# A two-layer sequence kernel: reciprocals of the softmax denominators stored once and repeated by a copy within DRAM

## Chip, cores and metric

The kernel runs on one core of a Trainium2 chip. The metric is the device time of one execution in microseconds (us). A core has a matrix engine (TensorE, "PE" in the profile, its weight loads "PEld"), a vector engine (DVE), a scalar engine (ACT), a general engine (GpSimd, "POOL") and a sequencer that issues nearly all transfers here (SyncE, "SP"). Transfers run on 16 DMA engines. "DRAM" is the chip's memory outside the core; on-chip tiles have 128 partitions.

## What is computed

Eight sequences (B = 8) of S = 512 rows by D = 256 pass through two layers. Layer 0 is a feed-forward block with one of eight weight sets for each sequence, a residual and a layer norm. Layer 1 is a conditioned transformer block with H = 16 heads of 16 columns. Cut to what the change touches:

```
scores = einsum('bhqd,bhkd->bhqk', q / sqrt(16), k) + attention_bias   # bias: 8 x 16 x 512 x 512 floats
probs  = softmax(where(src_mask, -inf, scores), axis=-1)
ctx    = einsum('bhqk,bhkd->bhqd', probs, v)
x      = x + (ctx @ Wo + bo)
h      = layernorm(x) * g2 + beta2
out    = x + gelu2(h @ W1 + b1) @ W2 + b2
```

The kernel does not divide `probs`. It sums exp(scores) through a 17th column of ones in `v`, so that `ctx` comes out undivided beside its denominators, and multiplies `ctx` by the reciprocals of the denominators later.

## The kernel before, in words

There are three stages. The first (about 0 to 260 us) is layer 0 and the projections to q, k and v. The second is the attention: N = 512 tiles, that is 128 units (a batch and a head) of 4 tiles of 128 query rows. All engines walk the same step number n. In step n PE makes the scores of tile n (L714, for every fourth unit with a second matmul L712), DVE adds the bias and finds the row minimum (L1257), ACT takes the exponential (L940), PE turns tile n-4 (L725, the constant LAG is 4), ACT or DVE copies it out of PSUM (L830, L1267), and later PE makes the context of four heads at once (L738). POOL adds the mask to the bias tile of three units in four, in two halves (L1455).

The third stage (from about 805 us) takes the batches one by one: POOL multiplies context by reciprocals (`divide`, L1491), ACT and POOL split the product in two parts (`high_c`, `low_c`), PE projects it (`project`), DVE adds the residual and norms, PE runs the two feed-forward matmuls (`up`, `down2`), and SP stores the output. PE's order in it is written out by hand: `up(b)`, `project(b + 2)`, three of four `down2(b)`, the turn of batch b + 1, the last `down2(b)`.

SP issues its transfers in one written order too, and a wait in it holds all that stands behind. `attention_loads(n)` is what it issues in step n. Those that matter here:

- `load_bias(u)`: 1 MB for unit u, 128 rows of 8 KB, into one of NB = 5 buffers. It stands in step 4(u - 3) and waits until PE has turned the last tile of unit u - 5, tile 4u - 17, which PE does in its step 4u - 13.
- `load_qk(g, i)`: q and k for a group of 8 units (32 tiles), in four pairs, in steps 4, 10, 16 and 22 of the 32 tiles before.
- `store_ctx(gi)`: in step 16 gi + 37, five transfers. Context of four heads to `sc_c` and the four rows of denominators to `sc_d`.
- For each batch b: `load_den(b)` in step 64 b + 97 loads the 16 x 512 denominators as a tile of 128 x 64; DVE takes reciprocals into `rr` (L1272); `store_rec(b)` in step 64 b + 111 writes `rr` to `sc_r[b]`, laid out [2, 16 columns, 8 heads, 512], which holds each reciprocal 16 times, once for each column of its head. It does so in two transfers (k = 0 and 1), each with 64 partitions of `rr` as source, 16 times over, 256 bytes a piece: 1024 pieces, 256 KB.
- `load_ctx(b)` loads `sc_c[b]` to `t_cin` and `sc_r[b]` to `t_din`, both 128 x 1024 (two pieces of 2 KB for each partition), waiting on the semaphore `d_rs` between the two. Batch 0's stands in step 486, batch 1's in step 498, batches 2 and 3 after step 515, batches 4 to 7 in the loop over the output batches. `load_x2(b)` brings the residual `t_rin`.

Batches 0 to 6 have `store_rec` in the second stage, batch 7 in the third. In the profile all of these stand as line L276, the helper `load`; they are told apart by their tensors. The shape of the source and destination lists is that of the lines quoted here:

```
for k in range(NK):
    load(d_rs, sc_r[b, k].rearrange("d h (c q) -> (h c) d q", c=8), rr[64 * k:64 * k + 64, :].unsqueeze(1).broadcast_to([64, HD, H * S // 128]))
```

Of the kernel before, what the change touches and what calls it, by code (L numbers as in the profile page):

```python
# [5 lines left out]
F32 = mybir.dt.float32  # L6
# [8 lines left out]
B, S, D, I, H, HD = 8, 512, 256, 1024, 16, 16  # L15
NT = S // 128
NK = D // 128
# [48 lines left out]
def kpn(a):  # L66
    return a.rearrange("(k p) n -> p k n", p=128)
# [41 lines left out]
def masks(u, half):  # L109

    return 2 * sum(on_pool(i) for i in range(u)) + half + 1


def program(nc, x, x_t, itok, tstep, bias, mask, Wi, bi, Wo0, bo0, gam, bet, Wada, bada, Wq, bq, Wk, bk, Wv, bv,
            Wo, bo, W1, b1, W2, b2, g2, be2, ident, freqs, out):
    with ExitStack() as ctx:

        def sem(name):
            return ctx.enter_context(nc.semaphore(name))

        def dram(name, shape, dt):
            return nc.dram_tensor(name, shape, dt, kind="Internal").ap()

        def sbuf(stack, name, shape, dt=F32):
            return stack.enter_context(nc.sbuf_tensor(f"t_{name}", shape, dt))
# [8 lines left out]

        sc_c = dram("sc_c", [B, NK, HD, H // NK, S], F32)

        sc_d, sc_r = dram("sc_d", [B, H, S], F32), dram("sc_r", [B, NK, HD, H // NK, S], F32)


        d_id, d_it, d_c, d_w, d_xt, d_wi, d_wo, d_v, d_ss, d_ssb = (sem(f"d_{n}") for n in ("id", "it", "c", "w", "xt", "wi", "wo", "v", "ss", "ssb"))  # L140
# [2 lines left out]
        d_p = [[sem(f"d_p{p}{n}") for n in range(2)] for p in range(2)]  # L143
        d_b = [sem(f"d_b{i}") for i in range(NB)]
        d_q, d_m, d_vb, d_cs = ([sem(f"d_{n}{i}") for i in range(2)] for n in ("q", "m", "vb", "cs"))
        d_cw, d_rb, d_dn, d_rs = (sem(f"d_{n}") for n in ("cw", "rb", "dn", "rs"))
        d_l, d_r, d_out = ([sem(f"d_{n}{i}") for i in range(2)] for n in ("l", "r", "out"))
        p_hid, p_down, p_x2T, p_q, p_v, p_emb = (sem(f"p_{n}") for n in ("hid", "down", "x2T", "q", "v", "emb"))
        a_gelu, a_hTh, a_xTh, a_wih, a_woh, a_x2Th, a_p0, a_p1, a_wsm, a_sin = (
# [21 lines left out]
        with ExitStack() as st:  # L171
# [20 lines left out]
            stt, mv, rs = sbuf(st, "stt", [128, NT, 6]), [sbuf(st, f"mv{i}", [128, NT, 2]) for i in range(2)], [sbuf(st, f"rs{i}", [128, NT]) for i in range(2)]  # L192
# [12 lines left out]
        with ExitStack() as st:  # L205
# [17 lines left out]
            dn, rr = (sbuf(st, n, [128, H * S // 128]) for n in ("dn", "rr"))  # L223
            ws = {"o": (Wo, NK, D), "1": (W1, NK, I), "2": (W2, NM, D)}
            wl = {n: [sbuf(st, f"cw{n}{p}", [128, k, w], F32R) for p in "hl"] for n, (_, k, w) in ws.items()}
            rb, b1c = sbuf(st, "rb", [128, 4, D]), sbuf(st, "b1c", [128, NM])
# [45 lines left out]
        def sync_program(e):  # L272
            P = Port(e)

            def load(signal, dst, src):
                e.dma_start(dst, src).then_inc(signal, 16)  # L276
# [80 lines left out]
            def store_part(b, n, a, mt):  # L357

                if a == 0:
                    P.wait_ge(a_p0, 4 * b + 2 * n + mt + 1)  # L360
                elif a == 1:
                    P.wait_ge(a_p1, 2 * b + n + 1)
                else:
                    P.wait_ge(g_p2, 2 * b + n + 1)
                g = slice(a, NP3, 3) if n else slice(3 * a, min(3 * a + 3, NP3))
                k = len(range(NP3)[g])
                load(d_p[b % 2][n], sc_qk[b, n, mt, g].rearrange("i p s -> p i s"), parts[b % 2][n][:, a:a + 1, mt, :].broadcast_to([128, k, S]))
# [26 lines left out]
            def load_bias(u):  # L394
                if u >= NB:
                    P.wait_ge(p_T, 4 * (u - NB) + 4)
                load(d_b[u % NB], bt[u % NB][:, :, :], bias[u // H, u % H])

            def load_qk(n, i):

                b, half = divmod(n, 2)
                hs = slice(2 * i, 2 * i + 2)
                P.wait_ge(p_sc, 32 * (n - 1))
                if b < 2 or n < 4:
                    for w in range(2):
                        P.wait_ge(d_p[b % 2][w], PT * (b // 2 + 1))
                for dst, w in ((qs, 0), (ks, 1)):
                    load(d_q[n % 2], dst[n % 2][:, hs, :], sc_qk[b, w, half].rearrange("i (d h) s -> (i d) h s", d=HD)[:, hs, :])
# [39 lines left out]
            def first_stage_over():  # L448
                P.wait_ge(v_v, 4 * B)
                P.wait_ge(g_p2, 2 * B)  # L450
                P.wait_ge(v_x2Tl, NK * B)

            def attention_loads(n):
                nonlocal nextb
                while nextb < min(UNITS, n // NT + NB) and n >= 4 * (nextb - NB) + 3 + LAG + 1:
                    load_bias(nextb)
                    nextb += 1
                if n in late_stores:
                    i = late_stores.index(n)
                    store_part(B - 1, i // 2 % 2, i // 4, i % 2)  # L460
                if n == 88:
                    first_stage_over()
                    for w in range(2):
                        P.wait_ge(d_p[0][w], PT * B // 2)
                    P.wait_ge(d_v, 16 * B)
                    P.wait_ge(d_x2[0], 16 * B // 2)
                    P.wait_ge(d_x2[1], 16 * B // 2)
                if n in load_w_at:
                    w, c = load_w_at[n]
                    a, _, wd = ws[w]  # L470
                    P.wait_ge(g_cw, w_chunks[w] + c)
                    if wd > 512:
                        load(d_cw, wf[:, :], kpn(a)[:, c * 512 // wd, c * 512 % wd:c * 512 % wd + 512])
                    else:
                        load(d_cw, wf[:, :].rearrange("p (k n) -> p k n", n=wd), kpn(a)[:, c * 512 // wd:(c + 1) * 512 // wd, :])
                if n == 236:
                    for w in range(2):
                        P.wait_ge(d_p[1][w], PT * B // 2)
                if n in ROWS_AT:
                    i = ROWS_AT.index(n)  # L480
                    if i < 4:
                        load(d_rb, rb[:, i, :], (bo, g2, be2, b2)[i].rearrange("(a n) -> a n", a=1).broadcast_to([128, D]))
                    else:
                        load(d_rb, b1c[:, :], b1)
                m = n % 32 - (4 if n > 32 else FIRST)
                step = QK_STEP if n > 32 else 1
                if n < N and 0 <= m < 4 * step and m % step == 0 and n // 32 + 1 < 2 * B:
                    if n == FIRST:
                        first_stage_over()
                    load_qk(n // 32 + 1, m // step)  # L490
                if n < N and n % 64 == (22 if n < 64 else 12) and n // 64 + 1 < B:
                    load_mask(n // 64 + 1)
                if n < N and n % 64 == 28 and n // 64 + 1 < B:
                    load_v(n // 64 + 1)
                if n == EARLY_C:

                    P.wait_ge(p_sc, N - 32)
                    P.wait_ge(p_pv, UNITS // 4 - 4)
                    P.wait_ge(g_M, masks(16 * (B - 1) - 2, 1))
                    load_ctx(0)  # L500

                if n == N - 14:
                    load_x2(0)
                    load_ctx(1)
                    load_x2(1)
                m = n - LAG - CLAG - 3 * PSTEP
                if 0 <= m - 4 < N and (m - 4) % 16 == 15:
                    store_ctx((m - 4) // 16)
                if 0 <= m - 16 < N - 64 and (m - 16) % 64 == 63:
                    load_den((m - 16) // 64)  # L510
                if 0 <= m - 30 < N - 64 and (m - 30) % 64 == 63:
                    store_rec((m - 30) // 64)

            def store_ctx(gi):
                b, hg = divmod(gi, 4)
# [10 lines left out]

            def store_rec(b):
                P.wait_ge(v_rc, b + 1)
                for k in range(NK):
                    load(d_rs, sc_r[b, k].rearrange("d h (c q) -> (h c) d q", c=8), rr[64 * k:64 * k + 64, :].unsqueeze(1).broadcast_to([64, HD, H * S // 128]))  # L530

            def load_ctx(b):

                P.wait_ge(g_cTl, b - 1)
                load(d_l[b % 2], ccs[b % 2][:, :, :], sc_c[b].rearrange("k d h s -> (d h) k s"))
                P.wait_ge(d_rs, 32 * (b + 1))
                load(d_l[b % 2], crr[b % 2][:, :, :], sc_r[b].rearrange("k d h s -> (d h) k s"))

            def load_x2(b):
# [27 lines left out]
                at += 1  # L567


            load_ctx(2)  # L570
            P.wait_ge(v_x3, 1)
            load_x2(2)
# [4 lines left out]
            for b in range(B):  # L577
                if b:
                    P.wait_ge(v_os, b)
                    load(d_out[(b - 1) % 2], rows(out[b - 1]), os_[(b - 1) % 2][:, :, :])  # L580
                if b == 1:
                    load_den(B - 1)
                if b == 3:
                    store_rec(B - 1)
                if b + 3 < B:
                    P.wait_ge(v_x3, b + 2)
                    load_x2(b + 3)
                if b + 4 < B:
                    load_ctx(b + 4)
            for i in range(2):  # L590
                hs = slice(2 * i, 2 * i + 2)
# [453 lines left out]
        def vector_program(e):  # L1045
            P = Port(e)
# [221 lines left out]

            def reciprocals(b):
                P.wait_ge(d_dn, 16 * (b + 1))  # L1270
                P.wait_ge(d_rs, 32 * b)
                e.reciprocal(rr[:, :], dn[:, :]).then_inc(v_rc, 1)  # L1272

            def attention(n):
# [333 lines left out]
```

## Time and profile before

| | |
|---|---|
| median of 3 runs | 1032.62 us (1030.04 to 1034.39) |
| the profiled execution, its own time | 1031.43 us |
| its span in the profile | 1029.7 us |
| what lies around the span | 1.7 us |
| busy: PE, PEld, DVE, ACT, POOL | 983.5, 735.7, 811.7, 770.7, 657.6 us |
| moved by DMA | 278.38 MB in 134866 packets |

The profile page divides the span into 40 slices. "GB/s" is what was moved in each. A row of the view by windows gives, for a stretch, the busy time of each engine with its instruction count in brackets, then the granted TensorE clock (1.00 is 2.4 GHz, 0.50 is 1.2 GHz), the mean busy share of the 16 DMA engines, and GB/s. A row of the view in order of time has start, duration, engine, line, operation, output <- input, count, and in brackets the idle time before it with what ended it. "To landing" is the time from a transfer's issue to its arrival.

### The profile page before, as it was taken

What the parts mean: (1) busy time and instruction counts of PE and PEld (TensorE: products, weight loads), DVE (VectorE), ACT (ScalarE), POOL (GpSimd) and SP (SyncE); (2) the same over time, 40 slices, a digit from 0 to 9 for tenths busy, and PEclk for the clock granted to TensorE, in tenths of its full rate; (3) what the DMA queues carried; (4) which work ended last, traced back from release to release, by engine and by line L of the source; (5) the groups of instructions that cost most, each with busy time, mean ns of one, the idle gap of its engine ahead of it and who ended that gap; (6) DMA issues with size and microseconds to landing.
All of it is one profiled execution on the core that took longest, in us unless ns stands there. A gap on an engine that the chain in (4) does not pass through costs nothing.

```text
span 1029.7 us, 19304 instructions
## 1 busy us (share of the span) xinstructions
PE 983.5 (96%) x6678; PEld 735.7 (71%) x6744; DVE 811.7 (79%) x1934; ACT 770.7 (75%) x1283; POOL 657.6 (64%) x349
## 2 busy tenths in 40 slices
PE   4999999999899998999999999999999899999998
PEld 3889988999565655555555565565656599998897
DVE  5599899997968887888988898888889665555563
ACT  5755575556689998999999999999999544444444
POOL 3466766764257786887878988788788744444210
PEclk9999999999999999999999999999999999999999
DMA  8747689879989999999999999999999412231001
GB/s 234 266 159 262 222 286 325 297 257 328 374 289 412 368 400 339 367 393 346 367 331 374 389 354 385 323 382 366 349 344 337 149 60 69 80 103 42 21 22 41
DMA packets 134866, 278.38 MB, mean 270 GB/s; under 512 B 29794, under 2 KB 85858, under 8 KB 118258
## 3 DMA queue, kind: packets, MB, share of 16 engines
q1 hardware_dynamic: 134770, 277.14, 75.4%
q8 instruction: 55, 0.90, 0.4%
q14 instruction: 41, 0.34, 0.1%
HBM read 222.03 MB, written 55.07 MB: 269 GB/s over the span
## 4 chain that ended last, share of the span: by engine, by line
PE 60%; ACT 23%; DMA 5%; DVE 4%; POOL 4%; issue 3%; SPq 1%; ACTq 0%; DVEq 0%; POOLq 0%
PE psO L609 17%; PE psH L609 16%; ACT t_bt L940 12%; PE psT L725 10%; ACT t_pt L830 6%; PE psS L714 5%; PE psV L738 4%; PE psQ L609 4%; DMA t_bt<-in_fside_Bx16xSxS 3%; POOL t_bt L1455 2%; PE psA L609 2%; DMA t_ks<-sc_qk 1%; ACT t_mb L962 1%; PE psS L712 1%; ACT t_cv L830 1%
## 5 line engine op out<-in xcount | busy, mean ns | idle before, releaser
L1455 POOL TENSOR_TENSOR t_bt<-t_bt,t_mb 128x1024 f32<-128x1024 f32 x182 | 385.0, 2146 | 100.7 <-DMA t_bt<-in_fside_Bx16xSxS 100.6
L1257 DVE CUSTOM_DVE_ANT_0 t_bt<-psS,t_bt 128x512 f32<-128x512 f32 x512 | 339.4, 686 | 72.7 <-PE psS L714 55.6
L940 ACT ACTIVATE t_bt<-t_bt,t_nm 128x512 f32<-128x512 f32 x512 | 357.8, 741 | 5.2 <-DVE t_nm L1257 5.0
L725 PE MATMUL psT<-t_idf,t_bt 128*128 128x128 f32 x2048 | 310.9, 275 | 9.9 <-ACT t_bt L940 8.0
L725 PEld LDWEIGHTS psT<-t_idf,t_bt 128*128 128x128 f32 x2048 | 250.5, 141 | 80.2 <-ACT t_bt L940 28.3
L830 ACT ACTIVATE t_pt<-psT 128x512 f32<-128x512 f32 x317 | 193.9, 612 | 20.3 <-PE psT L725 20.1
L714 PE MATMUL psS<-t_ks,t_qs 128*128 128x512 bf16 x482 | 183.8, 381 | 8.9 <-issue 4.1
L1267 DVE COPY t_pt<-psT 128x512 f32<-128x512 f32 x195 | 133.7, 686 | 1.9 <-PE psT L725 1.9
L738 PE MATMUL psV<-t_pt,t_vs 128*17 128x512 f32 x1024 | 134.8, 601 | 0.0
L714 PEld LDWEIGHTS psS<-t_ks,t_qs 128*128 128x128 bf16 x512 | 49.9, 98 | 83.6 <-DVE t_nm L1257 66.7
L867 ACT ACTIVATE psH<-psH,t_bi 128x512 f32<-128x512 f32 x64 | 42.3, 662 | 70.9 <-PE psH L609 67.9
L1057 DVE TENSOR_TENSOR t_chTl<-t_chf,t_chTh 128x512 fp32r<-128x512 f32 x64 | 51.8, 812 | 30.4 <-ACT t_chTh L830 30.4
L609 PE MATMUL psO<-t_cw2h,t_chTh 128*128 128x256 f32 x256 | 73.0, 285 | 0.0
L609 PE MATMUL psO<-t_woh,t_hTh 128*128 128x256 f32 x256 | 72.6, 284 | 0.0
L609 PE MATMUL psO<-t_woh,t_hTl 128*128 128x256 f32 x256 | 72.6, 283 | 0.0
L609 PE MATMUL psO<-t_wol,t_hTh 128*128 128x256 f32 x256 | 72.5, 283 | 0.0
L609 PE MATMUL psO<-t_cw2h,t_chTl 128*128 128x256 f32 x256 | 72.5, 283 | 0.0
L609 PE MATMUL psO<-t_cw2l,t_chTh 128*128 128x256 f32 x256 | 72.4, 283 | 0.0
L609 PE MATMUL psH<-t_xTh,t_wih 128*128 128x512 f32 x128 | 52.6, 411 | 13.9 <-DVE t_wil L1057 8.5
L1005 ACT ACTIVATE t_chf<-psH,t_b1c 128x512 f32<-128x512 f32 x64 | 43.8, 684 | 28.7 <-PE psH L609 27.4
L830 ACT ACTIVATE t_lTh<-psX 128x512 fp32r<-128x512 f32 x16 | 8.7, 595 | 75.5 <-PE psX L762 75.5
L1378 POOL TENSOR_TENSOR t_wol<-t_wo_f,t_woh 128x2048 fp32r<-128x2048 f32 (+1 forms) x9 | 34.9, 3879 | 36.9 <-DVE t_woh L1160 34.6
(174 smaller groups left out, 1930.0 us busy)
## 6 DMA issues: line engine op xcount, KB each, us to landing
t_bt<-in_fside_Bx16xSxS SPq DMA_DIRECT2D x128, 1024.0 KB, 8.2
sc_qk<-t_parts SPq DMA_DIRECT2D x64, 384.0 KB, 6.5
t_qs<-sc_qk SPq DMA_DIRECT2D x64, 256.0 KB, 6.4
t_ks<-sc_qk SPq DMA_DIRECT2D x64, 256.0 KB, 7.3
t_wo_f<-in_L_cond_Wo SPq DMA_DIRECT2D x8, 1024.0 KB, 6.1
sc_qk<-t_parts SPq DMA_DIRECT2D x32, 256.0 KB, 8.3
t_wi_f<-in_L_cond_Wi SPq DMA_DIRECT2D x7, 1024.0 KB, 8.8
sc_v<-t_v SPq DMA_DIRECT2D x8, 544.0 KB, 8.1
```

The lines of the kernel that those rows point to most:

```text
L609: ins = e.matmul(dst, lh[a], rh[c], start=n == 0, stop=n == last)
L714: e.matmul(s, qs[g % 2][:, h % 8, t * 128:(t + 1) * 128], ks[g % 2][:, h % 8, :], start=on_pool(u), stop=True).then_inc(p_sc, 1)
L725: ins = e.transpose(psT[turned_bank(n)][:, kk, :], bt[u % NB][:, t, kk * 128:(kk + 1) * 128], idf[:, :])
L738: ins = e.matmul(psV[32 * g:32 * g + VW, :], vs[b % 2][:, kk, u % H, :], pt[u % NP][:, kk, :], start=kk == 0, stop=kk == NT - 1)
L830: e.activation(dst, src, ACT.Copy).then_inc(signal, 1)
L867: e.activation(f[:, :], f[:, :], ACT.Gelu, bias=bis[b % 2][:, m:m + 1]).then_inc(a_gelu, 1)
L940: e.activation(p, p, ACT.Exp, bias=nm[:, n % NR:n % NR + 1], scale=-1.0).then_inc(a_exp, 1)
L1005: e.activation(f[:, :], psH2[m % 2][:, :], ACT.Gelu_apprx_sigmoid, bias=b1c[:, m:m + 1]).then_inc(a_gel2, 1)
L1057: e.tensor_tensor(dst, src, high.bitcast(F32), ALU.subtract).then_inc(signal, 1)
L1257: e.tensor_tensor_reduce(bt[u % NB][:, t, :], s, bt[u % NB][:, t, :], -1.0, 3.0e38, ALU.add, ALU.min, nm[:, n % NR:n % NR + 1]).then_inc(v ...
L1267: e.tensor_copy(pt[u % NP][:, :, t * 128:(t + 1) * 128], psT[turned_bank(n)][:, :, :]).then_inc(v_ev, 1)
L1455: e.tensor_tensor(bt[u % NB][:, hs, :], bt[u % NB][:, hs, :], mb[b % 2][:, hs, :], ALU.add).then_inc(g_M, 1)
```

## The change

`store_rec` writes the reciprocals once, 128 x 64 floats (32 KB), to a new DRAM tensor `sc_r1[b]` laid out [16 heads, 512]. A new step `spread_rec` copies `sc_r1[b]` to `sc_r[b]` within DRAM: for each half k of the heads a run of 4096 floats (16 KB), 16 times. It waits for the store (`d_rc`) and for the spread of the batch before (`d_rs`). For batches 0 and 1 it stands in steps 119 and 183 of the attention, for 2 and 3 behind step 515, for 4 to 7 in front of their `load_ctx` in the loop over the output batches. The store for batch 7 moves one output batch forward (b == 2). The reciprocal on DVE now waits for the single store (`d_rc`) of the batch before.

```
         sc_c = dram("sc_c", [B, NK, HD, H // NK, S], F32)
-        sc_d, sc_r = dram("sc_d", [B, H, S], F32), dram("sc_r", [B, NK, HD, H // NK, S], F32)
+        sc_d, sc_r1 = (dram(n, [B, H, S], F32) for n in ("sc_d", "sc_r1"))
+        sc_r = dram("sc_r", [B, NK, HD, H // NK, S], F32)
...
-        d_cw, d_rb, d_dn, d_rs = (sem(f"d_{n}") for n in ("cw", "rb", "dn", "rs"))
+        d_cw, d_rb, d_dn, d_rc, d_rs = (sem(f"d_{n}") for n in ("cw", "rb", "dn", "rc", "rs"))
...
                 if 0 <= m - 30 < N - 64 and (m - 30) % 64 == 63:
                     store_rec((m - 30) // 64)
+                if 0 <= m - 38 < 128 and (m - 38) % 64 == 63:
+                    spread_rec((m - 38) // 64)
...
             def store_rec(b):
                 P.wait_ge(v_rc, b + 1)
-                for k in range(NK):
-                    load(d_rs, sc_r[b, k].rearrange("d h (c q) -> (h c) d q", c=8), rr[64 * k:64 * k + 64, :].unsqueeze(1).broadcast_to([64, HD, H * S // 128]))
+                load(d_rc, sc_r1[b].rearrange("h (c q) -> (h c) q", c=8), rr[:, :])
+
+            def spread_rec(b):
+                P.wait_ge(d_rc, 16 * (b + 1))
+                P.wait_ge(d_rs, 16 * b)
+                load(d_rs, sc_r[b].rearrange("k d h s -> k d (h s)"), sc_r1[b].rearrange("(k h) s -> k (h s)", k=NK).unsqueeze(1).broadcast_to([NK, HD, H // NK * S]))
...
                 load(d_l[b % 2], ccs[b % 2][:, :, :], sc_c[b].rearrange("k d h s -> (d h) k s"))
-                P.wait_ge(d_rs, 32 * (b + 1))
+                P.wait_ge(d_rs, 16 * (b + 1))
                 load(d_l[b % 2], crr[b % 2][:, :, :], sc_r[b].rearrange("k d h s -> (d h) k s"))
...
+            spread_rec(2)
+            spread_rec(3)
             load_ctx(2)
             P.wait_ge(v_x3, 1)
             load_x2(2)
...
-                if b == 3:
+                if b == 2:
                     store_rec(B - 1)
                 if b + 3 < B:
                     P.wait_ge(v_x3, b + 2)
                     load_x2(b + 3)
                 if b + 4 < B:
+                    spread_rec(b + 4)
                     load_ctx(b + 4)
...
             def reciprocals(b):
                 P.wait_ge(d_dn, 16 * (b + 1))
-                P.wait_ge(d_rs, 32 * b)
+                P.wait_ge(d_rc, 16 * b)
                 e.reciprocal(rr[:, :], dn[:, :]).then_inc(v_rc, 1)
```

## Rows read from the trace of the kernel before

**Rows 1.** The page: GB/s in 40 slices of the span, and the queue of SP's transfers.

```profile
GB/s 234 266 159 262 222 286 325 297 257 328 374 289 412 368 400 339 367 393 346 367 331 374 389 354 385 323 382 366 349 344 337 149 60 69 80 103 42 21 22 41
...
q1 hardware_dynamic: 134770, 277.14, 75.4%
```

**Rows 2.** View by windows: a stretch of the attention, and one of the third stage.

```profile
600.00:650.00 50.00, 48.47 (x355) 30.01 (x360) 44.42 (x123) 48.37 (x88) 41.19 (x23) 1.00 0.99 373
...
850.00:900.00 50.00, 49.63 (x338) 45.45 (x337) 28.08 (x58) 21.99 (x35) 22.30 (x12) 1.00 0.24 74
```

**Rows 3.** Waits in the attention, 330 to 790 us: total us, times, longest.

```profile
POOL t_bt L1455 <- DMA t_bt<-in_fside_Bx16xSxS: 84.2, 46, 6.4
...
DVE t_bt L1257 <- POOL t_bt L1455: 3.4, 5, 1.0
```

**Rows 4.** SP's own waits, same stretch.

```profile
SPq L276 <- PE psT L725: 228.0, 92, 7.9
```

**Rows 5.** DMA issues of the whole run: count, KB each, median us to landing.

```profile
sc_r<-t_rr SPq DMA_DIRECT2D x16, 256.0 KB, 7.1
...
t_rin<-sc_x SPq DMA_DIRECT2D x8, 512.0 KB, 3.7
```

**Rows 6.** The bias tiles, 330 to 790 us: the mask add (ns), and landing.

```profile
L1455 POOL TENSOR_TENSOR t_bt<-t_bt,t_mb x170: 2121/2146/2173, 328.0 to 788.8; 128x1024 f32<-128x1024 f32 x170
...
DMA to landing us min/median/max: 5.0/8.1/11.9
```

**Rows 7.** SP in order of time, around batch 0's store of reciprocals.

```profile
388.68 5.51 SPq L276 DMA_DIRECT2D sc_r<-t_rr  x2
394.24 3.55 SPq L276 DMA_DIRECT2D t_bt<-in_fside_Bx16xSxS  x1
...
399.72 0.51 SPq L276 DMA_DIRECT2D t_bt<-in_fside_Bx16xSxS  x1
...
403.21 0.44 SPq L276 DMA_DIRECT2D t_ks<-sc_qk  x1
```

**Rows 8.** Waits, 400 to 416 us.

```profile
DVE t_bt L1257 <- PE psS L714: 6.2, 6, 2.3
...
PE psS L714 <- DMA t_ks<-sc_qk: 2.7, 1, 2.7
```

**Rows 9.** View by windows, 408 to 416 us.

```profile
408.00:416.00 8.00, 5.25 (x29) 2.85 (x28) 3.04 (x8) 4.50 (x9) 6.56 (x4) 0.79 1.04 423
```

**Rows 10.** SP in order of time: later stores of reciprocals (batches 1, 2 and 6).

```profile
458.46 2.85 SPq L276 DMA_DIRECT2D sc_r<-t_rr  x2
...
524.29 3.31 SPq L276 DMA_DIRECT2D sc_r<-t_rr  x2
...
782.81 3.15 SPq L276 DMA_DIRECT2D sc_r<-t_rr  x2
```

**Rows 11.** SP in order of time, start of the third stage, and batch 5's context.

```profile
792.43 1.83 SPq L276 DMA_DIRECT2D sc_c<-t_cv  x4
802.85 0.38 SPq L276 DMA_DIRECT2D t_cin<-sc_c  x1
...
856.36 0.37 SPq L276 DMA_DIRECT2D t_cin<-sc_c  x1
```

**Rows 12.** Loads of the repeated reciprocals: landing.

```profile
DMA to landing us min/median/max: 4.6/5.5/9.3
```

**Rows 13.** POOL in order of time: `divide` and `low_c` of batch 2, `divide` of batch 5.

```profile
819.04 2.43 POOL L1491 TENSOR_TENSOR t_cin<-t_cin,t_din 128x1024 f32<-128x1024 f32 x1
...
827.09 2.39 POOL L1378 TENSOR_TENSOR t_cTl<-t_cin,t_cTh 128x1024 fp32r<-128x1024 f32 x1 [3.26 <-ACT t_cTh L830]
...
893.23 2.40 POOL L1491 TENSOR_TENSOR t_cin<-t_cin,t_din 128x1024 f32<-128x1024 f32 x1
```

**Rows 14.** ACT in order of time: `high_c` of batch 2.

```profile
825.97 1.04 ACT L830 ACTIVATE t_cTh<-t_cin 128x1024 fp32r<-128x1024 f32 x1
```

**Rows 15.** PE in order of time: the first matmul of `project` for batch 2.

```profile
830.52 0.28 PE L609 MATMUL psA<-t_cwoh,t_cTh 128*128 128x256 f32 x1
```

More of the change, by code:

```diff
@@ L135, in program @@
         sc_c = dram("sc_c", [B, NK, HD, H // NK, S], F32)
-        sc_d, sc_r = dram("sc_d", [B, H, S], F32), dram("sc_r", [B, NK, HD, H // NK, S], F32)
+        sc_d, sc_r1 = (dram(n, [B, H, S], F32) for n in ("sc_d", "sc_r1"))
+        sc_r = dram("sc_r", [B, NK, HD, H // NK, S], F32)
         d_id, d_it, d_c, d_w, d_xt, d_wi, d_wo, d_v, d_ss, d_ssb = (sem(f"d_{n}") for n in ("id", "it", "c", "w", "xt", "wi", "wo", "v", "ss", "ssb"))
@@ L145, in program @@
         d_q, d_m, d_vb, d_cs = ([sem(f"d_{n}{i}") for i in range(2)] for n in ("q", "m", "vb", "cs"))
-        d_cw, d_rb, d_dn, d_rs = (sem(f"d_{n}") for n in ("cw", "rb", "dn", "rs"))
+        d_cw, d_rb, d_dn, d_rc, d_rs = (sem(f"d_{n}") for n in ("cw", "rb", "dn", "rc", "rs"))
         d_l, d_r, d_out = ([sem(f"d_{n}{i}") for i in range(2)] for n in ("l", "r", "out"))
@@ L512, in attention_loads @@
                     store_rec((m - 30) // 64)
+                if 0 <= m - 38 < 128 and (m - 38) % 64 == 63:
+                    spread_rec((m - 38) // 64)
             def store_ctx(gi):
@@ L528, in store_rec, with spread_rec @@
                 P.wait_ge(v_rc, b + 1)
-                for k in range(NK):
-                    load(d_rs, sc_r[b, k].rearrange("d h (c q) -> (h c) d q", c=8), rr[64 * k:64 * k + 64, :].unsqueeze(1).broadcast_to([64, HD, H * S // 128]))
+                load(d_rc, sc_r1[b].rearrange("h (c q) -> (h c) q", c=8), rr[:, :])
+            def spread_rec(b):
+                P.wait_ge(d_rc, 16 * (b + 1))
+                P.wait_ge(d_rs, 16 * b)
+                load(d_rs, sc_r[b].rearrange("k d h s -> k d (h s)"), sc_r1[b].rearrange("(k h) s -> k (h s)", k=NK).unsqueeze(1).broadcast_to([NK, HD, H // NK * S]))
             def load_ctx(b):
@@ L535, in load_ctx @@
                 load(d_l[b % 2], ccs[b % 2][:, :, :], sc_c[b].rearrange("k d h s -> (d h) k s"))
-                P.wait_ge(d_rs, 32 * (b + 1))
+                P.wait_ge(d_rs, 16 * (b + 1))
                 load(d_l[b % 2], crr[b % 2][:, :, :], sc_r[b].rearrange("k d h s -> (d h) k s"))
@@ L567, in sync_program @@
                 at += 1
+            spread_rec(2)
+            spread_rec(3)
             load_ctx(2)
@@ L582, in sync_program @@
                     load_den(B - 1)
-                if b == 3:
+                if b == 2:
                     store_rec(B - 1)
@@ L588, in sync_program @@
                 if b + 4 < B:
+                    spread_rec(b + 4)
                     load_ctx(b + 4)
@@ L1270, in reciprocals @@
                 P.wait_ge(d_dn, 16 * (b + 1))
-                P.wait_ge(d_rs, 32 * b)
+                P.wait_ge(d_rc, 16 * b)
                 e.reciprocal(rr[:, :], dn[:, :]).then_inc(v_rc, 1)
```

## The prediction

> **What bounds the kernel now.** I read the page first. In the second stage the slices carry 325 to 412 GB/s and in the third 21 to 103 [rows 1], so the change moves work from a stretch with busy DMA engines to one with idle ones. The view by windows says the same: at 600 to 650 us PE is busy for 48.5 of 50 us, ACT for 48.4, the DMA engines for a share of 0.99 at 373 GB/s; at 850 to 900 us PE has 49.6 of 50 and DMA a share of 0.24 [rows 2]. PE sets the pace of both stages, with ACT beside it in the attention.
>
> Does DMA cost time in the attention? The waits say little. POOL stood 84.2 us for bias tiles, but DVE, the next in line, stood only 3.4 us for POOL [rows 3], and SP itself stood 228.0 us waiting until PE had freed a bias buffer [rows 4]. The engines are well used, yet demand, not capacity, sets the rate. So 2.4 MB less to write in the attention (seven times 0.5 MB against seven times 32 KB and two of 0.5 MB) is worth nothing by itself; only lateness counts. A bias tile is asked for 13 steps before its unit's first scores. The four batches from 524.29 to 782.81 took 64.6 us each [rows 10], 1.01 us a step, so the lead is 13.1 us. POOL needs 2.1 us for the first half [rows 6], which leaves 11.0 us for the transfer. It lands in 8.1 us as the median, 5.0 at least [rows 6]: slack of 3 to 6 us.
>
> One place shows that slack used up. Batch 0's two stores hold SP for 5.5 us, the bias issue behind them for 3.6 more, and the last `t_ks` of the group leaves at 403.21 [rows 7]. PE waits 2.7 us for it and DVE 6.2 us for scores [rows 8], and from 408 to 416 us the granted clock is 0.79 [rows 9]: part of it was at 1.2 GHz, after PE had idled, worth 8 x 0.21 = 1.7 us. The store to the next batch's store takes 388.68 to 458.46, 69.8 us; the next gap is 65.8, the later ones 64.6 on average [rows 7, 10]. Batch 0's store costs about 5 us, batch 1's about 1, the others nothing.
>
> **Removed.** Seven pairs of stores leave the attention, and one the third stage. In exchange come stores of 32 KB in one issue. By the gaps above that gives 69.8 - 64.6 = 5.2 us, less a little for what else batch 0 has, say **-4.9**, and **-0.9** for batch 1 (65.8 against 64.9 as the gap if 0.3 of it is ordinary scatter). Bounds of the sum: -2 (the delay has other causes too, late `store_part`s among them) to -8 (0.4 us more from each of five other batches). DVE's reciprocal and its wait cost nothing: the store it waits for is 64 steps old.
>
> **Added: the copy.** 512 KB within DRAM, in two outer rows, each 16 pieces of 16 KB. No row shows such a transfer, nor how many of the 16 engines it gets. The price depends on that almost alone. All 16 engines together moved at most 412 GB/s in a slice [rows 1], 25.8 each; a busy engine in the third stage moved 74 / (16 x 0.24) = 19.3 [rows 2]. Spread over 16 engines the copy is 524288 B / 412 GB/s = 1.3 us (1.7 us at the lower rate). On two, one for each outer row, it is 262144 B / 25.8 = **10.2 us** (13.6 at the lower rate). Every large transfer of this kernel lists 64 or 128 rows; this one lists 2 on its outer index. I take that an engine gets whole outer rows, and so the two-engine end with the faster rate, as pieces here are long like the bias's, which make up that slice. The even spread is a rival.
>
> The Trainium skill, "DMA: Bandwidth & Descriptors", section "Why a DMA increments its semaphore by 16 and not by 1", states that the transfer is divided over the largest number of engines up to 16 that divides both lists' outermost count: here that gives two, on the lowest-numbered engines. By that rule the sum is the one below; with all 16 engines it would be that of rival (a). No row here shows it.
>
> *In the attention (batches 0 and 1).* The copy stands in step 119 (183), directly ahead of `load_bias(33)` (49) in step 120. The wait on `d_rc` is over by then: the store went 8 steps = 8.1 us earlier, and the old, larger ones landed in 7.1 [rows 5]. SP is not held; the two DMA engines are. Each bias tile is spread over all engines, and the share of it that falls to those two queues behind 10.2 us of copy. It lands after 8.1 + 10.2 = 18.3 us, 7.3 late against 11.0; with the shortest landing, 5.0 + 10.2, it is 4.2 late. Middle: 5.7 us. Both units are ones that POOL masks, so POOL waits, then DVE, then PE and ACT, which have no spare time to win it back. The tiles behind are late by the same amount and add nothing: 2 x 5.7 = **+11.4**. Such a stall was followed by the lower clock once [rows 9]: 2 x 1.7 = **+3.4**. Bounds: 2 x 1 (short backlog, slack of 6 us and some catching up) to 2 x (13.6 + 8.1 - 11.0 + 1.7) = 25.
>
> *At the start of the third stage (batches 2 and 3).* SP is free from 794.3 (end of the `sc_c` stores of batch 7's second group) to 802.85, when `low_c(0)` lets `t_cin` go [rows 11]. Copy 2 is issued at 794.3. The engines are behind then: `t_din`, issued shortly before, landed in 9.3 us [rows 12], where a lone load takes 3.7 [rows 5]; 3.7 less 1.3 us of data is 2.4 of latency, and 9.3 - 3.7 leaves 5.6 of queue, some 4 at 794.3. Landed: 794.3 + 4 + 2.4 + 10.2 = 810.9. Copy 3 waits for that on SP, and `load_ctx(2)` stands behind it: `t_cin` and `t_din` leave 8 us later than before and then queue behind copy 3 on its two engines: 811 + 2.4 + 10.2 + 2.5 (two loads of 32 KB an engine) = 826.1. `divide(2)` ran at 819.04 [rows 13], but `high_c(2)` not before 825.97 [rows 14], so there are 4.5 us of cover. From 826.1 `divide` ends at 828.5, and ACT is 2.5 us late with PE's `up` tiles behind it; add the bias add and `low_c` (2.4 us each on POOL): 833.3 against PE's need at 830.52 [rows 15], 2.8 late. The two overlap: **+2.8**. Bounds 0 (even spread) to 10 (13.6 us copies).
>
> *Later (4 to 7).* Each copy is issued with its own wait and holds SP until it lands, some 13 us; behind it stand `t_cin`, `t_din` and the next output store. `t_cin` of batch 5 left at 856.36 [rows 11] and was used at 893.23 [rows 13]: 37 us of cover. The output store, once in 27 us, is waited for by nobody for two batches. **0**; even with doubled copies it stays covered. The store for batch 7, one output batch earlier, follows its reciprocal at once: 0.
>
> **Sum.** -4.9 - 0.9 + 11.4 + 3.4 + 2.8 = **+11.8 us** on the profiled execution's 1031.43 (span 1029.7 and 1.7 around it), which is 1.2 below the median of three runs; I carry the difference over to the median: 1032.6 + 11.8 = **1044.4 us**.
>
> **Rivals.** (a) *The copy takes all 16 engines.* 1.3 us of every engine is less than half a bias tile, within the slack; the third stage has cover. Then only the removed terms stay: 1032.6 - 5.8 = 1026.8, between 1025 and 1030. For it: nothing shows the opposite; against it: only two outer rows. (b) *Two engines, hidden.* If the pair's backlog is small and the pipeline's tiles in flight soak up most of it, each copy costs 2 to 3 us and no clock drop follows: -5.8 + 5 + 1 gives 1033. For it: DVE hardly ever waits for POOL [rows 3]; against it: unit 33's tile is the very next issue. (c) *Reading and writing DRAM share an engine's rate*: copies of 20 us. Each is then 10 us later in the attention, and two chained ones delay `divide(2)` by 20: 11.8 + 20 + 20 gives 1084. The kernel has no transfer from DRAM to DRAM, so nothing speaks for or against it. The change does what it says: the repeated layout is what `load_ctx` still reads.
>
> **Numbers.** Forecast 0.60, (a) 0.21, (b) 0.13, (c) 0.06. The forecast's own range is 1037 to 1056. 8 in 10 need (b) and part of (a) too: 1026 to 1057. A measurement can tell about 0.5%, 5.2 us. Faster by more than that: two thirds of (a), 0.14. Within: the rest of (a), (b) and a little of the forecast's low end, 0.22. Slower: 0.64.
>
> **What would show it.** In the changed profile: seven short `sc_r1` stores and bias issues no longer of 3 us behind them; copies that land in about 13 us, not 4 to 6; a wait of DVE or POOL on bias near batch times 413 and 478 us with the clock below 1.00 after it; `divide(2)` about 7 us later against the start of the third stage, and PE idle for 2 to 3 us ahead of `project(2)`. A landing of the copies below 8 us would make the forecast wrong and (a) right; a landing of 13 us without those waits would be (b).

## The result, and the profile after

The changed kernel takes 1043.19 us as the median of four runs (1041.11 to 1045.03), the kernel before 1032.51 beside it: a ratio of 1.0113, 95% interval 1.0093 to 1.0134. The profiled execution has a span of 1043.2 us.

The page after has the GB/s of the slices and the queue of SP, to be set against [rows 1], and below it the waits from 330 to 795 us, against [rows 3]:

```profile
GB/s 233 265 154 284 220 291 286 317 257 352 346 323 409 379 382 375 299 379 289 335 343 358 348 353 372 353 333 382 322 346 336 117 116 102 103 102 41 21 22 41
...
q1 hardware_dynamic: 119554, 277.40, 74.3%
```

```profile
POOL t_bt L1465 <- DMA t_bt<-in_fside_Bx16xSxS: 95.5, 52, 9.7
...
DVE t_bt L1267 <- POOL t_bt L1465: 17.3, 6, 7.4
...
ACT t_bt L950 <- DVE t_nm L1267: 12.6, 3, 6.3
```

The bytes are the same (277.40 against 277.14 MB) in 15,000 fewer packets, and the third stage's slices 33 to 36 rose from 60-103 to 102-116 GB/s: work was moved as meant. But two slices of the attention, the 17th and the 19th, sank to 299 and 289 GB/s. That is not a busy memory system; it is one that waits. DVE now stands 17.3 us for POOL instead of 3.4, with 7.4 us as the longest wait, and ACT behind it 12.6 us in three waits, 6.3 us at most.

Where they are is seen on SP and POOL in order of time, to be set against [rows 7]. SP:

```profile
388.35 0.32 SPq L277 DMA_DIRECT2D sc_r<-t_rr  x1
391.80 0.33 SPq L277 DMA_DIRECT2D t_bt<-in_fside_Bx16xSxS  x1
...
398.90 0.45 SPq L277 DMA_DIRECT2D t_ks<-sc_qk  x1
399.39 0.67 SPq L277 DMA_DIRECT2D sc_r<-sc_r  x1
400.11 3.84 SPq L277 DMA_DIRECT2D t_bt<-in_fside_Bx16xSxS  x2
...
461.10 0.32 SPq L277 DMA_DIRECT2D sc_r<-t_rr  x1
...
534.72 0.32 SPq L277 DMA_DIRECT2D sc_r<-t_rr  x1
```

and POOL:

```profile
406.04 4.25 POOL L1465 TENSOR_TENSOR t_bt<-t_bt,t_mb 128x1024 f32<-128x1024 f32 x2 [1.83 <-DMA t_bt<-in_fside_Bx16xSxS]
417.79 12.66 POOL L1465 TENSOR_TENSOR t_bt<-t_bt,t_mb 128x1024 f32<-128x1024 f32 x6 [7.50 <-DMA t_bt<-in_fside_Bx16xSxS]
```

The good half is there: the store takes SP 0.3 us instead of 5.5, and `t_ks` leaves at 398.90 instead of 403.21. Then the copy goes out at 399.39, and the bias tile issued at 400.11, by itself in order and on time, lands 17.6 us later, as the tile view of `t_bt` for 399.8 to 401 us has it:

```profile
DMA to landing us min/median/max: 17.6/17.6/17.6
```

POOL starts on it at 417.79, 7.5 us after it had nothing else to do. In the same trace the semaphore of that bias tile is raised 16 times as it lands, which I read as once for each engine's share: fourteen times by 410.14, and the last two at 417.46 and 417.72. The copy ahead of it has only two such late increments, at 414.80 and 415.04. So two of the tile's sixteen shares came some 7 us late, and both after the copy had ended. The same happens 73 us later, where POOL stands 9.7 us. The gap from batch 0's store to batch 1's is 461.10 - 388.35 = 72.8 us, the next 73.6, then 64.6 (534.72 to 599.37), where they were 69.8, 65.8 and 64.6 [rows 7, 10]. The granted clock in the two places:

```profile
408.00:424.00 16.00, 9.83 (x66) 6.40 (x65) 7.96 (x22) 9.59 (x17) 8.50 (x5) 0.89 0.73 255
480.00:500.00 20.00, 14.36 (x88) 8.47 (x88) 10.88 (x30) 11.80 (x21) 9.52 (x6) 0.83 0.73 261
```

A clock of 0.89 over 16 us and 0.83 over 20 us is a part at 1.2 GHz each time after PE had idled: (1 - 0.89) x 16 x 2 = 3.5 us at that level after the first stall, (1 - 0.83) x 20 x 2 = 6.8 us after the second, and half of each given up at most. The DMA share is 0.73 in both, against 0.99 in an ordinary stretch [rows 2].

In the third stage, SP against [rows 11], POOL against [rows 13], ACT and PE against [rows 14, 15]:

```profile
802.62 17.40 SPq L277 DMA_DIRECT2D sc_r<-sc_r  x2
820.07 0.42 SPq L277 DMA_DIRECT2D t_cin<-sc_c  x1
820.53 0.47 SPq L277 DMA_DIRECT2D t_din<-sc_r  x1
```

```profile
835.47 2.92 POOL L1501 TENSOR_TENSOR t_cin<-t_cin,t_din 128x1024 f32<-128x1024 f32 x1 [5.83 <-DMA t_din<-sc_r]
...
841.15 2.83 POOL L1388 TENSOR_TENSOR t_cTl<-t_cin,t_cTh 128x1024 fp32r<-128x1024 f32 x1
```

```profile
844.03 0.39 PE L619 MATMUL psA<-t_cwoh,t_cTh 128*128 128x256 f32 x1 [0.86 <-POOL t_cTl L1388]
```

The two copies hold SP for 17.4 us (one issue, the wait until it has landed, the other issue), POOL stands 5.8 us for `t_din`, and `project(2)` waits 0.9 us for `low_c`, not the 2 to 3 us that the prediction named as a sign. In this execution the third stage also has a stretch of granted clock 0.79 (828 to 836 us). From the last score's row minimum to the end it takes 231.1 us, against 228.0 in the kernel before.

### The profile page after: what moved, and what is told of

Read it like the earlier page. It is cut to its first block, busy times and chain, and to the rows that moved or that the text cites. A ratio compares the mean times of both kernels' runs of the same rounds, so it can differ in the third digit from the quotient of the medians.

```text
span 1043.2 us, 19306 instructions
## 1 busy us (share of the span) xinstructions
PE 988.2 (95%) x6678; PEld 738.6 (71%) x6744; DVE 814.5 (78%) x1934; ACT 771.4 (74%) x1283; POOL 659.7 (63%) x349
## 3 DMA queue, kind: packets, MB, share of 16 engines
q1 hardware_dynamic: 119554, 277.40, 74.3%
## 4 chain that ended last, share of the span: by engine, by line
PE 59%; ACT 21%; DMA 8%; DVE 4%; SPq 3%; issue 3%; POOL 2%; DVEq 0%; ACTq 0%; POOLq 0%
PE psO L619 15%; PE psH L619 15%; ACT t_bt L950 11%; PE psT L735 11%; ACT t_pt L840 6%; PE psS L724 5%; PE psV L748 5%; PE psQ L619 4%; DMA t_bt<-in_fside_Bx16xSxS 3%; SPq L277 3%; PE psA L619 2%; DMA sc_r<-sc_r 2%; DMA t_din<-sc_r 1%; PE psS L722 1%; ACT t_mb L972 1%
## 5 line engine op out<-in xcount | busy, mean ns | idle before, releaser
L950 ACT ACTIVATE t_bt<-t_bt,t_nm 128x512 f32<-128x512 f32 x512 | 357.8, 740 | 17.3 <-DVE t_nm L1267 17.1
L724 PE MATMUL psS<-t_ks,t_qs 128*128 128x512 bf16 x482 | 184.6, 383 | 17.6 <-DVE t_nm L1267 12.3
L877 ACT ACTIVATE psH<-psH,t_bi 128x512 f32<-128x512 f32 x64 | 42.3, 662 | 70.1 <-PE psH L619 67.2
L1067 DVE TENSOR_TENSOR t_chTl<-t_chf,t_chTh 128x512 fp32r<-128x512 f32 x64 | 54.7, 858 | 31.4 <-ACT t_chTh L840 31.4
L619 PE MATMUL psH<-t_xTh,t_wih 128*128 128x512 f32 x128 | 52.8, 412 | 12.6 <-DVE t_wil L1067 8.5
```

The lines of the kernel that those rows point to most:

```text
L619: ins = e.matmul(dst, lh[a], rh[c], start=n == 0, stop=n == last)
L724: e.matmul(s, qs[g % 2][:, h % 8, t * 128:(t + 1) * 128], ks[g % 2][:, h % 8, :], start=on_pool(u), stop=True).then_inc(p_sc, 1)
L877: e.activation(f[:, :], f[:, :], ACT.Gelu, bias=bis[b % 2][:, m:m + 1]).then_inc(a_gelu, 1)
L950: e.activation(p, p, ACT.Exp, bias=nm[:, n % NR:n % NR + 1], scale=-1.0).then_inc(a_exp, 1)
L1067: e.tensor_tensor(dst, src, high.bitcast(F32), ALU.subtract).then_inc(signal, 1)
```

## The experiments

Each was timed beside the kernel before on the same chip, so each has its own ratio; that kernel's median was 1031.46 us beside the kernels with sixteen rows, with the two stages apart (first timing) and with half the columns; 1030.59 beside the copy behind the bias issue, the two on the old stores and the one without a copy; 1032.12 beside the quarters and the two repeats. Differences of a few tenths between medians of different groups mean nothing. The theory, Q: a copy with two outer rows runs on two of the 16 DMA engines, for 10 us each, and whatever share of a later transfer belongs to those two queues stands behind it.

### Sixteen rows instead of two

```
-load(d_rs, sc_r[b].rearrange("k d h s -> k d (h s)"), sc_r1[b].rearrange("(k h) s -> k (h s)", k=NK).unsqueeze(1).broadcast_to([NK, HD, H // NK * S]))
+load(d_rs, sc_r[b].rearrange("k d h s -> d k (h s)"), sc_r1[b].rearrange("(k h) s -> k (h s)", k=NK).unsqueeze(0).broadcast_to([HD, NK, H // NK * S]))
```

> The changed kernel, with one edit: the copy lists the 16 columns outermost instead of the two halves, so the same 32 pieces of 16 KB go to the same places from the same step, but in 16 outer rows of two pieces. Theory Q (the copy sits on two DMA engines and the bias tile's share on them queues behind it): on 16 engines it is 1.3 us of each. It lands in under 8 us in the attention, in 4 to 5 in the third stage, both stalls of 7 us and the 2.9 us of the third stage go, and the time is 1026 to 1029 us, 4 to 6 below the kernel before. Rival C (contention: half a MB read and half a MB written within DRAM in a stretch whose engines are 0.99 busy costs its time however it is divided): the stalls stay within 1 us of 7 each, the time is 1039 or more. Rival W (SP held by the wait between the copies and the loads): the third stage keeps its 2.9 us, the time is about 1030.

Measured: 1027.58 us, ratio 0.9961 (0.9949 to 0.9974). Same bytes, same pieces of 16 KB, same steps, same waits; only the order of two indices in the lists differs, and 15.6 us go with it (1043.19 to 1027.58). From 395 to 420 us DVE's longest wait for POOL is 0.6 us:

```profile
DVE t_bt L1267 <- POOL t_bt L1465: 0.9, 2, 0.6
```

The bias tile behind the copy lands in 10.9 us, and in the windows of the two stalls nothing is left of them (DMA share 1.00 and 0.99, clock 1.00):

```profile
408.00:424.00 16.00, 15.68 (x117) 9.65 (x118) 14.21 (x40) 15.14 (x28) 14.63 (x10) 1.00 1.00 378
480.00:500.00 20.00, 19.20 (x143) 11.91 (x144) 17.64 (x49) 19.27 (x34) 17.79 (x12) 1.00 0.99 377
```

Contention (C) is refuted. Rival W fails too: SP is still held for 8.7 us by the first two copies of the third stage, yet the stage takes 228.0 us, as in the kernel before. One part of the expectation was missed: the copy in the attention landed in 9.1 us, not in under 8. The transfer view for 842 to 860 us, third stage, gives the landing of a copy of batch 4 on 16 rows, beside a load of the same size:

```profile
t_rin<-sc_x SPq DMA_DIRECT2D x1, 512.0 KB, 3.7
sc_r<-sc_r SPq DMA_DIRECT2D x1, 512.0 KB, 4.7
```

In the changed kernel the copy of batch 4 leaves at 838.56 and `t_din`, which SP issues the moment it has landed, at 851.93: 13.4 us against 4.7, both right behind one 512 KB load and with little else queued.

```profile
838.56 0.64 SPq L277 DMA_DIRECT2D sc_r<-sc_r  x1
844.01 0.37 SPq L277 DMA_DIRECT2D t_cin<-sc_c  x1
851.93 0.36 SPq L277 DMA_DIRECT2D t_din<-sc_r  x1
```

How many engines carry the copy is seen where hardly anything else is moved. View by windows of the changed kernel:

```profile
842.00:844.00 2.00, 1.17 (x5) 0.59 (x4) 2.00 (x1) 1.17 (x2) 1.98 (x1) 1.00 0.13 57
848.00:851.00 3.00, 3.00 (x27) 3.00 (x27) 2.83 (x9) 0.00 (x0) 1.64 (x2) 1.00 0.13 55
```

A share of 0.13 of 16 engines is 2.1 of them, so two, and 55 GB/s is some 27 for each. The copy's 16 KB packets run from 841.4 to 851.6 us in the trace, two at a time: about 10 us for 262144 B an engine, as the forecast had it. Its semaphore gets two late increments (851.61 and 851.91), that of a 16-row copy in the attention sixteen (404.76 to 408.06). This also answers rival (c): at 26 to 27 GB/s an engine, no less than the 25.8 of the best slice, reading and writing DRAM does not halve an engine's rate here.

### The two stages apart

In the second kernel batches 0 and 1 keep two rows and the rest have sixteen; in the third it is the other way round.

```
-load(d_rs, <two rows>)
+if b < 2:
+    load(d_rs, <two rows>)      # third kernel: <sixteen rows>
+else:
+    load(d_rs, <sixteen rows>)  # third kernel: <two rows>
```

> The changed kernel, with the 16-row copy for batches 2 to 7 only; batches 0 and 1, in the attention, keep the two-row copy. Q: the attention keeps its two stalls of about 7 us, the third stage is as before (228.1 us from the last score's minimum to the end, against 231.0 in the changed kernel): 1043.2 - 2.9 = 1040.3 us. W: nothing changes, 1043. C: 1043.

> The other half: 16 rows for batches 0 and 1, two rows for batches 2 to 7. Q: no stall in the attention, the third stage keeps 2.9 us: 1027.5 + 2.9 = about 1030.5 us. The two halves' differences from the changed kernel (-2.9 here absent, -12 to -13 here) add up to that of the kernel with 16 rows everywhere. C: 1043.

Measured: 1043.95 us for the second (ratio 1.0126, 1.0095 to 1.0158) and 1027.79 for the third (0.9969, 0.9952 to 0.9986). Nearly the whole loss is that of the two copies in the attention. The six in the third stage cost 1027.79 - 1027.58 = 0.2 us by the medians and 0.8 by the ratios (0.9969 and 0.9961, each good to less than 2 us), not 2.8: both expectations missed by that term. The profile of the third kernel shows how the lateness is covered, where the kernel with two rows everywhere has a 5.8 us wait:

```profile
816.73 2.40 POOL L1504 TENSOR_TENSOR t_cin<-t_cin,t_din 128x1024 f32<-128x1024 f32 x1 [2.72 <-DMA t_din<-sc_r]
...
823.45 2.51 POOL L1391 TENSOR_TENSOR t_cTl<-t_cin,t_cTh 128x1024 fp32r<-128x1024 f32 x1 [1.50 <-ACT t_cTh L843]
```

`divide(2)` is 2.7 us late, yet POOL still waits for ACT ahead of `low_c`: the cover holds. From the last score's row minimum to the end its third stage takes 229.5 us against 228.0 with 16 rows, and the difference is no more than what a granted clock of 0.86 at 808 to 820 us gives up, 12 x 0.14 = 1.7 us, which the last experiment's kernel without any copy has as well.

To make sure of this term, the changed kernel and the second one were timed again side by side:

> The changed kernel once more, unedited, beside the next one on the same chip, to size the third stage's term. Q, with the two-row copies of the third stage costing 2.8 us: 2.8 us above the next kernel. If their lateness is mostly covered, as the kernels with 16 and two late rows suggested (1027.58 and 1027.79): within 1 us of it.

> The kernel with 16-row copies in the third stage alone, once more, beside the one before. Its third stage holds no wait of POOL for t_din; the attention keeps both stalls. 1043 less what the third stage's two-row copies cost: 1040.3 by my term, 1042 to 1043 if they are covered.

Measured: 1043.11 us (ratio 1.012, 1.0095 to 1.0146) and 1042.66 (1.0100, 1.0082 to 1.0118): 0.4 us apart by the medians, but 2.1 by the ratios, with intervals of some 2 to 3 us on either side of each: this pair alone can't tell 0.4 from 2.8. The repeated profile of the changed kernel has 15.3 us for SP's two copies instead of 17.4 and a wait for `t_din` of 3.7 instead of 5.8:

```profile
800.84 15.32 SPq L277 DMA_DIRECT2D sc_r<-sc_r  x2
```

```profile
831.96 2.41 POOL L1501 TENSOR_TENSOR t_cin<-t_cin,t_din 128x1024 f32<-128x1024 f32 x1 [3.67 <-DMA t_din<-sc_r]
...
837.12 2.85 POOL L1388 TENSOR_TENSOR t_cTl<-t_cin,t_cTh 128x1024 fp32r<-128x1024 f32 x1
```

Its third stage takes 228.5 us, 0.5 more than the kernel before. In the three kernels of the next sections, which all have two rows there, it takes 228.2, 228.5 and 228.2 us, so four of the six profiles with two rows in that stage put the cost at 0.2 to 0.5 us. The first profile's 231.1 us is 3.1 more, of which the clock of 0.79 over 8 us gives up at most 1.7. The two copies' time differs by 2 us between the two profiles, and the cover seems to end about there, with the first profile on the far side of it. That last step is a reading of the profiles; no experiment shows it.

### Half the columns on two engines

```
+if b < 2:
+    load(d_rs, <columns 8 to 15, as 8 outer rows>)
+    load(d_rs, <columns 0 to 7, as 2 outer rows>)
...                                 # batches 2 to 7: two rows, as in the changed kernel
```

> The changed kernel; for batches 0 and 1 the copy is cut in two halves by columns: columns 8 to 15 in 8 outer rows, then columns 0 to 7 in two outer rows. The bytes are the same, the two loaded engines get 5.1 us of the two-row half and 1.3 of the other, 6.4 instead of 10.2. Q: each stall shrinks by 3 to 4 us, from 7.1 to 3 to 4, and the clock may not drop after it: 1043.2 minus 6 to 9 = 1034 to 1037 us. C: same bytes, same stalls, 1043. That the stall is a matter of the first-come issue alone (any copy ahead of the bias costs 7): 1043.

Measured: 1033.82 us, ratio 1.0030 (1.0014 to 1.0047), inside the expected 1034 to 1037 but for 0.2. The same bytes on more engines cost 9.4 us less than in the changed kernel. The bias tile behind the first copy lands in 14.3 us, between 10.9 (16 rows) and 17.6 (two), and DVE's longest wait for POOL falls from 7.4 to 5.2 us:

```profile
DVE t_bt L1271 <- POOL t_bt L1469: 11.8, 5, 5.2
```

By the engine's load, 6.4 us in place of 10.2, it should have fallen by 3.8; it fell by 2.2. Direction and order of size are Q's.

### Behind the next bias issue instead of ahead of it

```
-if 0 <= m - 38 < 128 and (m - 38) % 64 == 63:
-    spread_rec((m - 38) // 64)
+if 0 <= m - 39 < 128 and (m - 39) % 64 == 63:
+    spread_rec((m - 39) // 64)
```

> The changed kernel with the two-row copies of batches 0 and 1 one step later, in step 120 (184), right behind the bias issue of unit 33 (49) instead of right ahead of it. Q: the next bias tile, for unit 34 (50), is issued one unit (4.04 us) later and waits for what is left of the copy, so the stall shrinks by about 4 us from 7.1 to about 3, twice: 1043.2 - 8 = about 1035 us. C: the traffic is the same four microseconds later, 1043. If any stall of this sort costs the same once PE idles and the clock drops: 1040.

Measured: 1041.95 us, ratio 1.0104 (1.0077 to 1.0132). The expectation failed: 1.2 us less, not 8. The stall is as long and only one unit later, as POOL shows:

```profile
406.39 8.47 POOL L1465 TENSOR_TENSOR t_bt<-t_bt,t_mb 128x1024 f32<-128x1024 f32 x4 [2.04 <-DMA t_bt<-in_fside_Bx16xSxS]
422.91 4.21 POOL L1465 TENSOR_TENSOR t_bt<-t_bt,t_mb 128x1024 f32<-128x1024 f32 x2 [8.04 <-DMA t_bt<-in_fside_Bx16xSxS]
```

The error was to count only the later due time (4.04 us) of the tile behind. In a queue the tile for unit 34 has the same work ahead of it in either order: the tile for 33 and the copy. One bias tile is 64 KB an engine, 2.5 us, so passing it gains 4.04 - 2.5 = 1.5 us at the very best, and SP issued the copy 1.8 us later (401.23 against 399.39), so little is left to gain. The failure fits queued work and does not fit a plain delay of the neighbour, but it fits contention as well; the case against contention rests on the kernels with 16 rows and with halves, and on the increments above.

### Quarters, 16 steps apart

```
-if 0 <= m - 38 < 128 and (m - 38) % 64 == 63:
-    spread_rec((m - 38) // 64)
+for q in range(4):
+    if 0 <= m - 38 - 16 * q < 128 and (m - 38 - 16 * q) % 64 == 63:
+        spread_rec((m - 38 - 16 * q) // 64, q)   # 4 columns, 2 outer rows
```

> The changed kernel; for batches 0 and 1 the two-row copy is cut in four of 4 columns each (128 KB, still two outer rows), 16 steps apart (steps 119, 135, 151, 167 and 64 later). Bytes and outer rows are as in the changed kernel, so by contention (C) or by two engines as such the cost stays, about 16 us in the attention and 1043 us in all. By queued work (Q): 64 KB a piece and engine are 2.5 us ahead of the next bias tile, within its slack of 3 us, and 16 steps are enough to work most of it off (the engines moved 365 of 412 GB/s, so 16 us leave 1.8 us of spare time): stalls of 0 to 1 us each, at most 2 late in the row; 1029 to 1033 us.

Measured: 1034.82 us, ratio 1.0023 (1.0011 to 1.0036). More than half of the loss is gone (6.4 us above the 16 rows' ratio instead of 15.7), so it is not two engines as such, but 2 to 6 us more is left than I expected. The landing of the bias tiles issued from 433 to 470 us shows why; the first line is this kernel, the second the one with 16 rows:

```profile
DMA to landing us min/median/max: 10.9/12.7/13.3
```

```profile
DMA to landing us min/median/max: 5.7/7.6/9.5
```

The tiles land some 5 us later for the eight of them issued from 434 to 466 us; by the account above it is the two engines that stay behind. The spare capacity that I had worked out from 365 of 412 GB/s was not there: in the kernel before the DMA share was 0.97 to 1.01 in the 50 us stretches from 300 to 750 us, whether the rate was 354 or 384 GB/s. The lateness comes as many small waits, DVE waiting for POOL 11 times, 11.6 us in all and 3.4 at most, in place of two waits of 7.

### The old stores: batch 0 alone, and all but batch 0

In the first, only batch 0 stores once, with a copy on 16 rows; in the second, all but batch 0.

```
 def store_rec(b):
     P.wait_ge(v_rc, b + 1)
+    if b == 0:                      # second kernel: if b > 0
+        load(d_rc, sc_r1[b].rearrange("h (c q) -> (h c) q", c=8), rr[:, :])
+        return
     for k in range(NK):
...
```

> The kernel before with batch 0 alone changed: its reciprocals are stored once and copied in 16 rows; batches 1 to 7 keep the old pair of stores. It measures my term of -4.9 us for batch 0's old stores. If they hold SP and make t_ks late, as I read it, the gap from batch 0's to batch 1's store falls from 69.8 to about 65 and the time is 1032.5 - 4.9 = 1027.6 us. If that delay has other causes (late stores of q and k parts, the weight pieces), the time stays at 1031 to 1032.5.

> The complement: batch 0 keeps the old pair of stores, batches 1 to 7 are stored once and copied in 16 rows. It measures what the other batches' old stores cost: by my term 0.9 us for batch 1 and nothing for the rest, so 1031.6 us, at most 4 us less if each of them costs some tenths. Batch 0's gap stays at 69.8.

Measured: 1028.02 us (ratio 0.9971, 0.9957 to 0.9985) and 1031.21 (1.0008, 0.9992 to 1.0025). On this chip the kernel before took 1030.59 us, so the single stores gain 2.6 us for batch 0 and nothing that can be measured for the rest; the first kernel met its absolute time (1027.6), but its gain is half of the 4.9 us that was to be tested. Its gap shrinks only where it is changed; the first two lines are the first kernel, 65.5 us apart, the others the second, 70.1 and 65.2:

```profile
390.99 0.32 SPq L277 DMA_DIRECT2D sc_r<-t_rr  x1
...
456.44 3.79 SPq L277 DMA_DIRECT2D sc_r<-t_rr  x2
```

```profile
388.53 4.76 SPq L277 DMA_DIRECT2D sc_r<-t_rr  x2
458.62 0.32 SPq L277 DMA_DIRECT2D sc_r<-t_rr  x1
523.85 0.32 SPq L277 DMA_DIRECT2D sc_r<-t_rr  x1
```

### No copy at all

```
-spread_rec(b)   # at all its places, and sc_r itself
...
-load(d_l[b % 2], crr[b % 2][:, :, :], sc_r[b].rearrange("k d h s -> (d h) k s"))
+for k in range(NK):
+    load(d_l[b % 2], crr[b % 2][:, k, :], sc_r1[b, 8 * k:8 * k + 8, :].unsqueeze(0).broadcast_to([HD, H // NK, S]))
```

> The reciprocals are stored once, there is no copy, and the load of the third stage reads each head's row 16 times itself: two loads for each batch, 128 rows of 2 KB each, source repeated over the columns. The tensor sc_r is gone, with 4 MB written and 1 MB read in the attention for it. Q: same as 16 rows everywhere or a little better, 1026 to 1028.5 us; nothing it saves beyond that lies on the path. A gain of over 1 us on 16 rows everywhere would say that the even copies still cost something in the attention.

Measured: 1027.37 us, ratio 0.9963 (0.9951 to 0.9975), equal within the intervals to the copy on 16 rows (0.9961) with 4.2 MB less written. Both beat the kernel before and the changed one. In its profile the clock is 0.86 at 808 to 820 us, with no copy about:

```profile
808.00:820.00 12.00, 9.64 (x44) 7.74 (x44) 7.38 (x14) 4.95 (x8) 7.85 (x4) 0.86 0.46 138
```

## Why the prediction held, by its steps

**The price of the copy.** Forecast 10.2 us an engine, landing in some 13; measured about 10 us of packets and a landing in 13.4 with little queued, 15.6 in the attention and 16.7 for the first copy of the third stage, which was forecast at 16.6. The choice of two engines over sixteen, open in the rows of before, is shown three ways: by the pair of kernels that differ in nothing else, by a DMA share of 0.13 while the copy runs alone, and by its two late increments. By the rule of the Trainium skill, "DMA: Bandwidth & Descriptors", section "Why a DMA increments its semaphore by 16 and not by 1", two rows give two engines and sixteen rows sixteen; the runs agree: 13.4 against 4.7 us.

**The stalls in the attention.** Forecast 5.7 us of lateness and 1.7 of clock each, 14.8 in all. Against the kernel with 16 rows, whose gaps are 65.6 and 65.2 us, the changed kernel's 72.8 and 73.6 are 7.2 and 8.4 longer: 15.6. Of these the clock is at most 1.7 and 3.4 us, half of the 3.5 and 6.8 us at 1.2 GHz. The split was thus 10.5 and 5.1 instead of 11.4 and 3.4. The landing of the bias tile was forecast at 18.3 with the median and 15.2 with the least landing; it was 17.6.

**The removed stores.** Forecast -4.9 and -0.9. By the gaps, 69.8 to 65.6 and 65.8 to 65.2 with 16 rows: -4.2 and -0.6. By the times it is 3.9 us for all (0.9961), and in another group 2.6 (1028.02 against 1030.59) for batch 0 alone. The term was right in place and 1 to 2 us too large in size.

**The third stage.** Forecast +2.8; by the medians of two pairs 0.2 and 0.4, by their ratios 0.8 and 2.1, by the third stage's length 0.2 to 0.5 in the four profiles with two rows there and no low clock. This is the term that was most mis-sized. The second pair alone would not show it; the first pair and these lengths do. The lateness itself came as worked out (a wait of POOL for `t_din` of 2.7, 3.7 and 5.8 us in three profiles), but the cover, which I put at 4.5 us on `divide`, was near its edge, and my sum took landings on the far side of it. Of the 3.1 us that the first profile shows, up to 1.7 is lower clock, which the profiles of the second kernel, with 16 rows in that stage, and of the kernel without a copy have as well.

**Sum.** Forecast 1044.4 us, measured 1043.19. The measured terms, -3.9 + 15.6 + 0.3, give +12.0 against a forecast of +11.8; the errors cancelled (removal 1.9 too large, third stage about 2.5 too large, attention 0.8 too small), and it is luck that the sum hit closer than its terms. The medians of the first comparison give +10.7 (1043.19 - 1032.51), those of the repeated one +11.0: within the intervals. One reading was off and changed nothing: the lowest slice of the ordinary attention is 323 GB/s, not 325, and slice 12 at the start of that stage has 289 [rows 1].

**Rivals.** (a), sixteen engines, is what the kernel with 16 rows became: 1027.58 measured, 1026.8 forecast. (b), hidden on two engines, fell with POOL's waits of 7.5 and 9.7 us. (c), half rate, fell with 13.4 us.

## What to carry to other kernels

In this kernel a transfer's price was not its bytes but the bytes on its busiest DMA engine, and its harm was done to the next transfers with little slack, not to itself. Put a large index outermost in both lists of a copy, above all when a repeat (step 0) tempts to put a count of two there; in this kernel that reordering alone turned 1.1% slower into 0.4% faster. Before adding anything to a saturated queue, work out the lead of the tile behind it, its usual landing and the difference; moving the addition by one place in the queue gained 1.2 us, cutting it in four gained 8.4 but left many small waits, and spreading it over all engines gained 15.6.

## What was not expected

The backlog persists: in the kernel with quarters the bias tiles issued over more than 30 us landed in 12.7 us instead of 7.6, although the stage's mean rate (362 GB/s at 340 to 780 us in the kernel before) is 12% under the best slice. And the start of the third stage sits at the edge of a clock drop: between 808 and 836 us 5 of the 13 profiles have a stretch at 1.2 GHz (0.86 over 12 us in one) and the others none, with and without copies, at a cost of 1.5 us (229.5 against 228.0 us). In the 6 us that begin 12 us after the last row minimum, where the drop begins when it comes, PE is busy for only 3.6 to 3.7 us in every one of them, so the idle time there does not tell which will drop; what does stays open.
